# First expert layer: activations transposed in 64-row pieces, two row halves of the array at once, into one pair of banks

## Chip, cores and metric

One core of a Trainium2 chip runs the whole program. The metric is the device time of one execution in microseconds (us); lower is better. All data is float32 unless a row says otherwise.

## What is computed

A small network over 8 x 192 tokens of width 192: an embedding, a recurrent layer, a first mixture of experts, a linear attention and a second mixture of experts. The change lies in the first mixture of experts, whose reference, cut to what matters, is

```python
def _L0_ffn_ref(x, router_w, router_b, w1, b1, w2, b2):     # x: 1536 tokens x 192
    ...
    topk_probs, topk_idx = jax.lax.top_k(probs, 2)          # 2 of 8 experts for each token
    ...
    for e in range(NUM_EXPERTS):
        h = jax.nn.gelu(flat_x @ w1[e] + b1[e], approximate=False)   # 192 -> 288
        y = h @ w2[e] + b2[e]                                        # 288 -> 192
        out = out + y * gates[:, e:e + 1]
```

## The kernel before, in words

The kernel is written engine by engine; each engine's instructions run in the order of its code, and engines wait for each other through semaphores (`wait_ge`, `then_inc`). The first expert stage is `experts(0, ...)` on each engine. The routed rows (3072 of them, padded for each expert to whole groups of 64) are worked through in 28 tiles (`NT0`) of 128 rows. The lower 64 rows of a tile belong to one expert, the upper 64 rows to the same or another one.

For tile `i` the steps are:

- GpSimd gathers the tile's 128 rows of 192 numbers into one of four places of `xs` (line 747).
- `t_x(i)` on TensorE (lines 1982 to 2003) turns them over, in two transposes of 128 rows x 96 columns (line 1988); tiles alternate between bank 0 and bank 1. VectorE copies the result to `xTs` (`evac_x`, line 1608).
- `g1` (lines 2012 and 2015) multiplies by the first weights. The 64 rows of the one expert use the array's columns 0 to 63, those of the other columns 64 to 127; two such matmuls run as a pair. ScalarE applies gelu (line 1033).
- `t_h(i)` (line 2038) turns the 288 hidden numbers over, in three transposes of 128 x 96; tiles alternate between banks 4 and 5. VectorE copies to `hTs` (`evac_h`, line 1633).
- `g2` (lines 2058 and 2061) multiplies by the second weights, VectorE copies the 192 results out (`evac_y`, line 1642), and GpSimd scatters them to DRAM (line 755).

The order on TensorE is written out by hand (lines 2086 to 2096). An iteration `i` is `t_x(i + 3)`, `t_h(i)`, `g1(i + 2)`, `g2(i - 1)`; the last iterations lack `t_x`, and the last two `g1`. On VectorE an iteration is `evac_x(i + 3)`, `evac_h(i)`, `evac_y(i - 1)` (lines 1659 to 1665). On ScalarE it is a copy of the upper half's first weights (line 1064), gelu, and a copy of the upper half's second weights (line 1073). On GpSimd it is the gather of tile `i + 7`, then the scatter of tile `i` (lines 781 to 784). TensorE's sequencer also loads each tile's expert number (line 1980).

The second expert stage, `experts(1, ...)`, already turns its rows over in 64-row pieces, in `t_x`'s other branch (line 1999): piece `a` lies in array rows 64a to 64a + 63 and writes bank `a` of a pair of neighbouring banks, `two_banks[...]`. A tile name such as 64\*96 in the profile says how many array rows and columns an instruction uses: 128\*96 uses all rows, 96\*64 half the columns, 64\*96 and 64\*128 half the rows.

After the stage everything waits for its last scatter: the rows are read back (`load_acc`, line 552), and normalization, attention and the second expert stage follow.

Of the kernel before, what the change touches and what calls it, by code (L numbers as in the profile page):

```python
# [33 lines left out]
P = 128  # L34
# [5 lines left out]
KC = 96  # L40
NK = D // KC
# [8 lines left out]
GR = 64  # L50
NT0 = -(-(NTOK * TOPK // GR + NE - 1) * GR // P)
# [26 lines left out]
C_ID, C_IOTA, C_MASK = 0, P, 2 * P  # L78
# [23 lines left out]
def build(nc, x, out):  # L102
    ctx = ExitStack()
    with ctx:
# [29 lines left out]
        con = sb("con", [P, NCONST])  # L134
        ident = con[:, C_ID:C_ID + P]
# [68 lines left out]
        xTs = sb("xTs", [P, 2, NK, P])  # L204
# [138 lines left out]
        hact2 = carve(reg3, HID1).rearrange("p (b f) -> p b f", b=2)  # L343
        hTs = carve(reg3, HID1).rearrange("p (b f) -> p b f", b=2)

        hT2 = reg3[:, 0:2 * HID1].rearrange("p (b f) -> p b f", b=2)
        xs = carve(reg3, RING * D2).rearrange("p (s n) -> p s n", s=RING)
# [3 lines left out]
        bank = [psum[:, 512 * i:512 * (i + 1)] for i in range(8)]  # L351
        two_banks = [psum[:, 1024 * i:1024 * (i + 1)].rearrange("p (s c) -> p s c", s=2) for i in range(4)]
# [66 lines left out]


        X_BANKS = (0, 2)

        Y_BANKS = ((6, 7), (0, 1))

# [769 lines left out]
        def _(dve):  # L1194
            link = Chain(dve, dve_self)
            V = nc.vector
# [130 lines left out]
            for r, (minus, plus) in enumerate(((1, 4), (6, 9), (8, 2))):  # L1327
                s = (r + 2) % 3
                V.tensor_tensor(entries(0, minus), S.vv[:, r], S.qk[:, s], ALU.subtract)
                ins = V.tensor_tensor(entries(0, plus), S.vv[:, r], S.qk[:, s], ALU.add)  # L1330
# [269 lines left out]
            def experts(l, hid, hc):  # L1600
                nhc = hid // hc

                def evac_x(i, p):

                    dve.wait_ge(tx_mm, l * NT0 + i + 1)
                    if l == 0:
                        src = bank[p][:, 0:2 * P].rearrange("p (k t) -> p k t", k=NK)
                        V.tensor_copy(xTs[0:KC, p, :, :], src[0:KC]).then_inc(tx_ev, 1)  # L1608
                    else:
                        dst = xT64[:, p, :, :].rearrange("p k (s t) -> p k s t", s=2)  # L1610
                        src = two_banks[X_BANKS[i == 1]]

                        row = xs[:, i % RING, DX:D2]
                        link(V.tensor_tensor(gs[:, i:i + 1], row[:, 0:1], sel[:, 0, i:i + 1], ALU.mult))
                        V.scalar_tensor_tensor(out=gs[:, i:i + 1], in0=row[:, 1:2], scalar=sel[:, 1, i:i + 1],
                                               in1=gs[:, i:i + 1], op0=ALU.mult, op1=ALU.add)
                        for k in range(NK3):
                            ins = V.tensor_scalar(dst[:, k], src[:, :, 64 * k:64 * k + 64], gb2[:, 0, k:k + 1],  # L1618
                                                  gb2[:, 1, k:k + 1], ALU.mult, ALU.add)
                        ins.then_inc(tx_ev, 1)  # L1620

                def copy_w(i, p):


                    e = dve.value_load(et[0:1, i:i + 1], min_val=0, max_val=NE - 1)
                    V.tensor_copy(w1r[:, p, 0:W1R // 2],
                                  w1b.rearrange("p e f -> p (e f)")[:, bass.ds(e * W1R, W1R // 2)]
                                  ).then_inc(w1r_dve, 1)

                def evac_h(i, p):  # L1630

                    dve.wait_ge(th_mm, l * NT0 + i + 1)
                    V.tensor_copy(hTs[0:hc, p, 0:nhc * P], bank[4 + p][0:hc, 0:nhc * P]).then_inc(th_ev, 1)

                def evac_y(i):
                    s = i % YRING
                    dve.wait_ge(g2_mm, l * NT0 + i + 1)
                    if i >= YRING:

                        dve.wait_ge(scat[s], 16 * turns(l, i, YRING))  # L1640
                    if l == 0:
                        V.tensor_copy(ys[:, s, :], bank[6 + i % 2][:, 0:D]).then_inc(y_ev, 1)  # L1642
                    else:
                        y0, y1 = (bank[b][:, 0:D] for b in Y_BANKS[i == NT - 1])
                        link(V.tensor_scalar(ys[:, s, :], y0, gs[:, i:i + 1], None, ALU.mult))  # L1645
                        V.scalar_tensor_tensor(out=ys[:, s, :], in0=y1, scalar=gs[:, i:i + 1],
                                               in1=ys[:, s, :], op0=ALU.mult, op1=ALU.add).then_inc(y_ev, 1)

                if l:
                    dve.wait_ge(ld_ffn1, 16 * 4 * NE)  # L1650
                for p in range(2):
                    if l:
                        copy_w(p, p)
                    evac_x(p, p)

                if l == 0:

                    evac_x(2, 0)
                    for i in range(NT0):
                        if i + 3 < NT0:  # L1660
                            evac_x(i + 3, (i + 1) % 2)
                        evac_h(i, i % 2)
                        if i >= 1:
                            evac_y(i - 1)
                    evac_y(NT0 - 1)
                    return

                for i in range(NT):
                    if i + 2 < NT:
                        evac_x(i + 2, i % 2)  # L1670
                        copy_w(i + 2, i % 2)
                    evac_y(i)
# [194 lines left out]
        def _(pe):  # L1867
# [105 lines left out]
            def experts(l, hid, hc, w1, w2, biased):  # L1973
                nhc = hid // hc
# [7 lines left out]
                def t_x(i):  # L1982

                    s = i % RING
                    pe.wait_ge(xs_ready[s], 16 * (turns(l, i, RING) + 1))
                    if l == 0:
                        for k in range(NK):
                            ins = nc.tensor.transpose(bank[s % 2][0:KC, k * P:(k + 1) * P],
                                                      xs[:, s, k * KC:(k + 1) * KC], ident)
                    else:  # L1990


                        if i >= 2:
                            pe.wait_ge(tx_ev, NT0 + (i if i > 2 else 1))
                        dst = two_banks[X_BANKS[i == 1]]
                        for k in range(NK3):
                            for a in range(2):
                                rs = slice(64 * a, 64 * a + 64)
                                ins = nc.tensor.transpose(
                                    dst[:, a, 64 * k:64 * k + 64],  # L2000
                                    xs[rs, s, 64 * k:64 * k + P],
                                    con[rs, C_ID + 64 * a:C_ID + 64 * a + 64])
                    ins.then_inc(tx_mm, 1)
# [29 lines left out]

                def t_h(i, p):

                    pe.wait_ge(act_done, l * NT0 + i + 1)
                    for c in range(nhc):
                        ins = nc.tensor.transpose(bank[4 + p][0:hc, c * P:(c + 1) * P], hact2[:, p, c * hc:(c + 1) * hc], ident)
                    ins.then_inc(th_mm, 1)

                def g2(i, p, e):
# [515 lines left out]
```

## Time and profile before

| | |
|---|---|
| runs | 447.07, 447.06, 449.86 us; median 447.07 |
| the profiled execution, its own time | 444.51 us |
| its span, first to last instruction | 442.7 us |
| granted TensorE clock, mean | 0.97 of full speed |
| busy share of the span | TensorE 93%, weight loads 68%, VectorE 65%, ScalarE 52%, GpSimd 50% |
| the first expert stage in the span | about 135.5 us (first transpose) to 218 us (last scatter landed) |

A row of the timeline gives the start in the span, the duration, engine, line, operation, output and inputs, and a count; rows of one line that follow each other are merged, and then the duration goes from the first start to the last end. Brackets give idle time before the instruction and what ended it. PE is TensorE, PEld its weight loads, DVE VectorE, ACT ScalarE, POOL GpSimd. Matmul durations overlap, since the next matmul starts while the one before drains; what a matmul costs is read from the distance between starts. A float32 matmul appears as two matmuls in the trace, a transpose as one.

### The profile page before, as it was taken

The page shows a single profiled execution, that of the slowest core. Times are in us where ns is not written, and L with a number is a line of the kernel's source. Part 1 is how long each engine was busy: PE and PEld are TensorE (multiplying, and loading weights), DVE is VectorE, ACT ScalarE, POOL GpSimd, SP SyncE. Part 2 cuts the span into 40 slices and gives each one's busy share as a digit, 9 for nine tenths or more (in the row PEclk, how much of TensorE's full clock was granted, in tenths as well). Part 3 has the DMA queues.
Part 4 walks back from the last instruction along what each step waited for, and adds up shares of the span by engine and source line. Part 5 has one row for each costly group of instructions (what it writes and reads, how often), then busy time and mean ns, then how long its engine had stood idle before and what let it go on. Part 6 is the DMA issues. An engine that isn't in the chain of part 4 may idle for free.

```text
span 442.7 us, 10871 instructions
## 1 busy us (share of the span) xinstructions
PE 411.5 (93%) x3803; PEld 302.7 (68%) x3803; DVE 288.7 (65%) x1345; ACT 230.6 (52%) x427; POOL 219.5 (50%) x260
## 2 busy tenths in 40 slices
PE   9999998989879999999889889968999999999993
PEld 6653755637535666666534469635999999999993
DVE  6789999999883444444496248995465565565651
ACT  1487845441764555555235203754666666665650
POOL 5303797798045677774400001425556657566534
PEclk9999699999989999999889999988999999999998
DMA  8709300010132222221299993093233333333313
GB/s 234 107 17 250 69 1 2 1 36 1 64 112 62 64 72 73 72 72 44 87 293 230 225 224 117 18 191 108 52 53 54 58 62 52 60 59 52 51 21 36
DMA packets 38584, 38.27 MB, mean 86 GB/s; under 512 B 7331, under 2 KB 35793, under 8 KB 38517
## 3 DMA queue, kind: packets, MB, share of 16 engines
q1 hardware_dynamic: 27601, 22.84, 22.5%
q0 software_dynamic: 9024, 13.44, 16.0%
q10 hardware_dynamic: 1906, 1.30, 1.0%
q8 instruction: 31, 0.51, 0.5%
q14 instruction: 22, 0.18, 0.1%
HBM read 27.72 MB, written 10.53 MB: 86 GB/s over the span
## 4 chain that ended last, share of the span: by engine, by line
DMA 23%; PE 12%; DVE 8%; issue 5%; ACT 2%; POOLq 1%; POOL 1%; DVEq 0%; ACTq 0%
DMA out<-a,idx 21%; PE bank L2029 2%; DVE h L1701 2%; PE bank L2308 1%; PE bank L1874 1%; PE bank L2068 1%; DVE st L1218 1%; PE bank L2417 1%; PE bank L2340 1%; DMA a<-expert_rows 1%; PE bank L2314 1%; PE bank L2389 1%; ACT reg L1022 1%; PE bank L2362 1%; POOL out L767 1%
## 5 line engine op out<-in xcount | busy, mean ns | idle before, releaser
L767 POOL DMA_INDIRECT out<-a,idx x31 | 50.7, 1634 | 46.3 <-DMA out<-a,idx 32.7
L747 POOL DMA_INDIRECT reg<-xn_rows,idxs x59 | 57.7, 978 | 29.4 <-issue 16.2
L2029 PE MATMUL bank<-reg,xT 64*128 64x128 f32 x1116 | 69.0, 275 | 1.3 <-DVE reg L1618 1.3
L2029 PEld LDWEIGHTS bank<-reg,xT 64*128 64x128 f32 x1116 | 65.0, 188 | 1.4 <-DVE reg L1618 1.4
L2068 PE MATMUL bank<-reg 64*128 64x192 f32 x744 | 65.4, 323 | 0.0
L2068 PEld LDWEIGHTS bank<-reg 64*128 64x128 f32 x744 | 59.8, 187 | 0.0
L1874 PE MATMUL bank<-con 128*128 128x512 bf16 x201 | 54.1, 428 | 0.0
L1054 ACT ACTIVATE reg<-reg 128x1152 f32 x31 | 36.1, 1163 | 33.8 <-PE bank L2068 33.8
L1645 DVE TENSOR_SCALAR a<-bank,gs 128x192 f32<-128x192 f32 x31 | 12.9, 417 | 53.3 <-PE bank L2068 53.3
L1874 PEld LDWEIGHTS bank<-con 128*128 128x128 bf16 x201 | 21.4, 110 | 27.3 <-issue 11.5
L755 POOL DMA_INDIRECT expert_rows<-a,idx x28 | 27.6, 987 | 22.0 <-DVE a L1642 21.7
L1642 DVE COPY a<-bank 128x192 f32<-128x192 f32 x28 | 10.0, 357 | 40.7 <-PE bank L2061 40.7
L1073 ACT ACTIVATE xT<-reg 97x576 f32 x28 | 19.1, 682 | 31.1 <-PE bank L2061 31.1
L2012 PE MATMUL bank<-reg,xTs 96*64 (+1 forms) x112 | 33.2, 419 | 0.4 <-DVE xTs L1608 0.4
L2015 PE MATMUL bank<-xT,xTs 96*64 96x288 f32 (+1 forms) x112 | 33.2, 419 | 0.0
L1618 DVE TENSOR_SCALAR reg<-bank,gb 128x128 f32<-128x128 f32 x93 | 32.3, 403 | 0.0
L2058 PE MATMUL bank<-reg 96*64 x168 | 31.9, 326 | 0.0
L2061 PE MATMUL bank<-xT,reg 96*64 96x192 f32 x168 | 31.9, 326 | 0.0
L716 POOL TENSOR_TENSOR reg<-reg 128x128 f32<-128x128 f32 x63 | 26.1, 454 | 5.2 <-PE bank L2189 4.9
L796 POOL TENSOR_SCALAR onep<-rs 128x3 f32<-128x3 f32 x4 | 0.9, 230 | 56.0 <-DVE nm L1230 56.0
L2058 PEld LDWEIGHTS bank<-reg 96*64 96x64 f32 x168 | 22.7, 136 | 7.7 <-issue 0.4
L1037 ACT ACTIVATE reg<-bank 128x384 f32<-128x384 f32 x31 | 15.2, 491 | 18.9 <-PE bank L2029 18.9
(370 smaller groups left out, 880.1 us busy)
## 6 DMA issues: line engine op xcount, KB each, us to landing
reg<-in_w2b SPq DMA_DIRECT2D x8, 576.0 KB, 10.6
reg<-in_w1b SPq DMA_DIRECT2D x8, 288.0 KB, 10.7
reg<-in_w1a SPq DMA_DIRECT2D x8, 216.0 KB
reg<-in_w2a SPq DMA_DIRECT2D x8, 216.0 KB
xn_rows<-xn SPq DMA_DIRECT2D x4, 384.0 KB, 2.8
reg<-in_w1b SPq DMA_DIRECT2D x8, 192.0 KB, 8.2
xn_rows<-xn SPq DMA_DIRECT2D x1, 1152.0 KB, 7.2
out<-h SPq DMA_DIRECT2D x1, 1152.0 KB
```

The lines of the kernel that those rows point to most:

```text
L747: pool.indirect_dma_start(xs[:, i % RING, 0:(D, D2)[l]], None, xd[l], bass.IndirectOffsetOnAxis(ap=idxs[:, i:i + 1], axis=0)).then_inc(xs_ ...
L755: pool.indirect_dma_start(ybuf, bass.IndirectOffsetOnAxis(ap=idx2[:, i:i + 1], axis=0), ys[:, i % YRING, :], None).then_inc(scat[i % YRING ...
L767: pool.indirect_dma_start(out, bass.IndirectOffsetOnAxis(ap=idx2[:, i:i + 1], axis=0), ys[:, i % YRING, :], None, compute_op=ALU.add).then ...
L1054: nc.scalar.activation(w2r[:, p, :], w2b.rearrange("p e c n -> p (e c n)")[:, bass.ds(e * W2R, W2R)], ACT.Copy).then_inc(w2r_act, 1)
L1618: ins = V.tensor_scalar(dst[:, k], src[:, :, 64 * k:64 * k + 64], gb2[:, 0, k:k + 1], gb2[:, 1, k:k + 1], ALU.mult, ALU.add)
L1874: MM(bank[bk][:, :], con[:, 0:P // 2].bitcast(BF16), con[:, 0:2 * P].bitcast(BF16), start=True, stop=True)
L2012: MM(bank[2 + p][0:GR, 0:hid], xTs[0:r, p, k, 0:GR], w1v[0:r, bass.ds(e * (NK * hid) + k * hid, hid)], start=(k == 0), stop=(k == NK - 1))
L2015: ins = MM(bank[2 + p][GR:P, 0:hid], xTs[0:r, p, k, GR:P], w1u[0:r, i % 3, k * hid:(k + 1) * hid], start=(k == 0), stop=(k == NK - 1))
L2029: ins = MM(bank[2 + 2 * p + a][:, c * P:(c + 1) * P], w1r[rs, p, col:col + hc], xT64[rs, p, k, :], start=(c == 0 and k == 0), stop=(c == n ...
L2058: MM(bank[6 + p][0:GR, 0:D], hTs[0:r, p, c * P:c * P + GR], w2v[0:r, bass.ds(e * (nhc * D) + c * D, D)], start=(c == 0), stop=(c == nhc - 1))
L2061: ins = MM(bank[6 + p][GR:P, 0:D], hTs[0:r, p, c * P + GR:(c + 1) * P], w2u[0:r, i % 2, c * D:(c + 1) * D], start=(c == 0), stop=(c == nhc ...
L2068: ins = MM(bank[Y_BANKS[i == NT - 1][a]][:, 0:D], hT2[rs, p, c * P:(c + 1) * P], w2r[rs, p, c * D:(c + 1) * D], start=(c == 0), stop=(c == ...
```

## The change

Each transpose of the first stage becomes two: the lower 64 rows in array rows 0 to 63, the upper 64 rows in array rows 64 to 127, each against its own 64 x 64 part of the identity, with 64 moving columns instead of 128. The lower halves write the first bank of a pair, the upper halves the second. The rows use banks 0 and 1 for every tile but tile 1, which uses banks 4 and 5; the hidden values use banks 4 and 5 for every tile. Where tiles took turns at two places, there is now one place, so `t_x(i)` waits for the copy of the tile before, and so does `t_h(i)`. VectorE's two copies keep their sizes, and read both banks in pieces of 64.

```diff
         X_BANKS = (0, 2)
+        XF_BANKS = (0, 2)
+        H_BANKS = 2
...
                     if l == 0:
-                        src = bank[p][:, 0:2 * P].rearrange("p (k t) -> p k t", k=NK)
-                        V.tensor_copy(xTs[0:KC, p, :, :], src[0:KC]).then_inc(tx_ev, 1)
+                        src = two_banks[XF_BANKS[i == 1]][0:KC, :, 0:NK * GR].rearrange("p s (k t) -> p k s t", k=NK)
+                        V.tensor_copy(xTs[0:KC, p, :, :].rearrange("p k (s t) -> p k s t", s=2), src).then_inc(tx_ev, 1)
...
-                    V.tensor_copy(hTs[0:hc, p, 0:nhc * P], bank[4 + p][0:hc, 0:nhc * P]).then_inc(th_ev, 1)
+                    V.tensor_copy(hTs[0:hc, p, 0:nhc * P].rearrange("p (c s t) -> p c s t", c=nhc, s=2),
+                                  two_banks[H_BANKS][0:hc, :, 0:nhc * GR].rearrange("p s (c t) -> p c s t", c=nhc)
+                                  ).then_inc(th_ev, 1)
...
                     if l == 0:
+                        if i >= 2:
+                            pe.wait_ge(tx_ev, i if i > 2 else 1)
+                        dst = two_banks[XF_BANKS[i == 1]]
                         for k in range(NK):
-                            ins = nc.tensor.transpose(bank[s % 2][0:KC, k * P:(k + 1) * P],
-                                                      xs[:, s, k * KC:(k + 1) * KC], ident)
+                            for a in range(2):
+                                rs = slice(GR * a, GR * a + GR)
+                                ins = nc.tensor.transpose(dst[0:KC, a, GR * k:GR * k + GR],
+                                                          xs[rs, s, k * KC:(k + 1) * KC],
+                                                          con[rs, C_ID + GR * a:C_ID + GR * a + GR])
...
                 def t_h(i, p):
 
-                    pe.wait_ge(act_done, l * NT0 + i + 1)
+                    pe.wait_ge(act_done, i + 1)
+                    if i >= 1:
+                        pe.wait_ge(th_ev, i)
                     for c in range(nhc):
-                        ins = nc.tensor.transpose(bank[4 + p][0:hc, c * P:(c + 1) * P], hact2[:, p, c * hc:(c + 1) * hc], ident)
+                        for a in range(2):
+                            rs = slice(GR * a, GR * a + GR)
+                            ins = nc.tensor.transpose(two_banks[H_BANKS][0:hc, a, GR * c:GR * c + GR],
+                                                      hact2[rs, p, c * hc:(c + 1) * hc],
+                                                      con[rs, C_ID + GR * a:C_ID + GR * a + GR])
                     ins.then_inc(th_mm, 1)
```

On TensorE, one iteration in the steady part of the stage, before (line 1980 loads the expert number, 1988 is `t_x`, 2038 is `t_h`, 2012 and 2015 are `g1`):

```order
L1980 TENSOR_LOAD et
L1980 ISA x2
L1988 MATMUL bank<-con,reg 96x128 [waits xs_ready1]
L1988 MATMUL bank<-con,reg 96x128
L2038 MATMUL bank<-con,reg 96x128 [waits act_done]
L2038 MATMUL bank<-con,reg 96x128 x2
L2012 ISA [waits w1r_act,tx_ev]
```

The same place in the changed kernel (1997 is `t_x`, 2052 is `t_h`, 2022 begins `g1`):

```order
L1984 TENSOR_LOAD et
L1984 ISA x2
L1997 MATMUL bank<-con,reg 96x64 [waits tx_ev,xs_ready1]
L1997 MATMUL bank<-con,reg 96x64 x3
L2052 MATMUL bank<-con,reg 96x64 [waits th_ev,act_done]
L2052 MATMUL bank<-con,reg 96x64 x5
L2022 ISA [waits w1r_act,tx_ev]
```

Five transposes of 128 columns have become ten of 64, the first of each group has one more wait, and nothing else on the engine has another place.

Near the start of the stage on TensorE, the third tile's transposes and the products of the second tile behind them, before:

```order
L1988 MATMUL bank<-con,reg 96x128 [waits xs_ready2]
L1988 MATMUL bank<-con,reg 96x128
L2012 ISA [waits w1r_act,tx_ev]
L2012 MATMUL bank<-reg,xTs 64x288
L2015 MATMUL bank<-xT,xTs 64x288
```

And in the changed kernel:

```order
L1997 MATMUL bank<-con,reg 96x64 [waits tx_ev,xs_ready2]
L1997 MATMUL bank<-con,reg 96x64 x3
L2022 ISA [waits w1r_act,tx_ev]
L2022 MATMUL bank<-reg,xTs 64x288
L2025 MATMUL bank<-xT,xTs 64x288
```

This is the first place with the new wait (here for the first tile's copy); the first two tiles have two different pairs of banks and wait for their rows alone, as before.

## Rows read from the trace of the kernel before

**Rows 1.** Spans and granted clock of the core

```profile
core 0: 442.7 us, clock 0.970
```

**Rows 2.** Busy time by stretch: us, each engine busy (instructions), granted clock, DMA share, GB/s

```profile
140.00:150.00 10.00, 10.00 (x89) 6.51 (x88) 4.42 (x12) 5.00 (x10) 4.91 (x5) 1.00 0.17 52
...
190.00:200.00 10.00, 10.00 (x95) 6.72 (x92) 3.99 (x10) 5.67 (x12) 7.04 (x8) 1.00 0.25 70
```

**Rows 3.** Timeline of TensorE, one iteration of the stage's steady part

```profile
168.53 0.33 PE L2058 MATMUL bank<-reg 97*64 x1
...
168.70 0.32 PE L2058 MATMUL bank<-reg 97*64 x1
...
168.96 0.42 PE L1988 MATMUL bank<-con,reg 128*96 128x128 f32 x2
169.22 0.49 PE L2038 MATMUL bank<-con,reg 128*96 128x128 f32 x3
169.64 0.46 PE L2012 MATMUL bank<-reg,xTs 96*64 x1
...
170.67 0.33 PE L2058 MATMUL bank<-reg 96*64 x1
...
171.75 0.42 PE L1988 MATMUL bank<-con,reg 128*96 128x128 f32 x2
```

**Rows 4.** The stage's transposes by line: duration in ns min/median/max, first and last start

```profile
L1988 PE MATMUL bank<-con,reg x56: 272/273/316, 135.7 to 205.3; 128*96 128x128 f32 x56
...
L2038 PE MATMUL bank<-con,reg x84: 272/273/317, 139.6 to 212.3; 128*96 128x128 f32 x84
```

**Rows 5.** Timeline of the other engines in the same iteration

```profile
169.08 0.36 DVE L1642 COPY a<-bank 128x192 f32<-128x192 f32 x1 [1.55 <-PE bank L2061]
169.42 0.42 DVE L1608 COPY xTs<-bank 96x256 f32<-96x256 f32 x1
169.72 0.99 POOL L755 DMA_INDIRECT expert_rows<-a,idx  x1 [0.52 <-DVE a L1642]
169.76 0.54 DVE L1633 COPY reg<-bank 96x384 f32<-96x384 f32 x1
170.41 0.39 ACT L1033 ACTIVATE reg<-bank 128x288 f32<-128x288 f32 x1
171.01 0.97 POOL L747 DMA_INDIRECT reg<-xn_rows,idxs  x1 [0.30 <-issue]
```

**Rows 6.** Timeline at the stage's two ends, and the chain that ended last behind it

```profile
136.72 0.45 PE L2012 MATMUL bank<-reg,xTs 96*64 x1 [0.39 <-DVE xTs L1608]
212.08 0.54 PE L2038 MATMUL bank<-con,reg 128*96 128x128 f32 x3
...
212.55 0.38 PE L2058 MATMUL bank<-reg 96*64 x1
...
215.70 2.34 DMA expert_rows<-a,idx
```

**Rows 7.** Second expert stage: its 64-row transposes, timeline and durations in ns

```profile
312.25 0.35 PE L1999 MATMUL bank<-con,reg 64*128 64x64 f32 x6
312.44 2.23 PE L2029 MATMUL bank<-reg,xT 64*128 64x128 f32 x36
...
L1999 PE MATMUL bank<-con,reg x186: 216/222/274, 304.1 to 425.7; 64*128 64x64 f32 x186
```

**Rows 8.** Attention: matmuls of 64 rows by 96 columns, timeline and durations in ns

```profile
256.35 0.59 PE L2368 MATMUL bank<-reg 64*96 64x102 f32 x8
256.87 1.32 PE L2340 MATMUL bank<-reg 128*96 128x256 f32 x5
...
L2368 PE MATMUL bank<-reg x32: 245/248/325, 247.4 to 270.4; 64*96 64x102 f32 x32
```

**Rows 9.** DMA issues: queue, operation, count, median us from issue to landing

```profile
reg<-xn_rows,idxs POOLq DMA_INDIRECT x59, 2.8
```

## The prediction

> **What bounds the kernel now.** First the granted clock of the whole span: 0.970, so the TensorE clock is rarely held back [rows 1]. Then the stretches of the first expert stage: TensorE is busy in all of 10 us out of 10, at clock 1.00 (the 2.4 GHz level), while VectorE has 4.0 to 4.4, ScalarE 5.0 to 5.7 and GpSimd 4.9 to 7.0; the stretches between these two read alike [rows 2]. So TensorE ends last in this stage, and what counts is the distance between the starts of its instructions. One iteration, from `t_x` to the next `t_x`, goes from 168.96 to 171.75, 2.78 us [rows 3]. The other engines' rows of the same iteration show that each waits for TensorE: VectorE sits idle 1.55 us for `g2`, GpSimd 0.52 us for the copied results [rows 5]. Behind the stage the chain that ended last goes through its last scatter [rows 6], and all that follows hangs on that; so a microsecond saved on TensorE here should come out at the end of the program.
>
> **What an iteration's transposes cost.** From the first start of `t_x` to the first start of `g1` it is 169.64 - 168.96 = 0.68 us [rows 3]. Inside, from merged rows: the two of `t_x` last 0.42 from the first start to the second's end, and one lasts 0.272 [rows 4], so the second starts at 169.11, 0.15 behind the first; `t_h` starts 0.11 later; its three last 0.49, so its two inner distances are (0.49 - 0.273)/2 = 0.109 each. `g1` starts 0.20 behind the last. So the pace is 0.109 per transpose, five make 0.545, and 0.135 is paid for entering (0.04) and leaving (0.09). Before them it is 0.26 from the last pair of `g2`, against 0.17 within `g2` [rows 3], again 0.09 more.
>
> **What they will cost.** Five transposes become five pairs of half the rows and half the moving columns. The trace has such pairs: in the second expert stage six pieces (three pairs) take from 312.25 to 312.44 up to the next line's start, 0.19, or 0.063 a pair; their own starts, (0.35 - 0.222)/2 = 0.064 a pair, agree [rows 7]. That is the dear end for a pair; the cheap end is half of 0.109, 0.054, if only the moving columns count. The pieces here hold 96 columns and not 128, so I go between: 0.060. The cost of entering and leaving I leave as it is: the attention's matmuls on 64 rows by 96 columns sit between other shapes, and leave for the next with (0.59 - 0.248)/3 = 0.114 a pair at most inside, the last starting at 256.69, and 256.87 - 256.69 = 0.18 behind it, 0.09 above the 0.087 that 102 columns need by 0.109 x 102/128 [rows 8]. It is the same 0.09 as here. So each transpose saves 0.109 - 0.060 = 0.049 us, and an iteration five of these, 0.245: 2.78 becomes 2.54.
>
> **The sum.** There are 56 transposes in `t_x` and 84 in `t_h` [rows 4], 140. The two of tile 1 lie in the shadow of VectorE's first copy, for which `g1` of tile 0 waits 0.39 us [rows 6]. In the last iterations `t_h` stands alone, 0.47 from its start to `g2`, and TensorE goes on without a gap there too [rows 6]. So 138 x 0.049 = 6.8 us; with 0.063 it is 138 x 0.046 = 6.3, with 0.054 it is 7.6.
>
> **The added waits cost nothing.** `t_x(i + 3)` now waits for `evac_x(i + 2)`, queued behind it `t_h`, `g1` and `g2` of the iteration. That copy begins at 169.42 and ends at 169.84, the next `t_x` is at 171.75: 1.9 us to spare, about 1.7 when the iteration is 0.24 shorter. `t_h(i)` waits for `evac_h(i - 1)`, done at 169.76 + 0.54 = 170.30 [rows 5], and the next `t_h` is at about 172.00, 1.7 to spare, about 1.4 after the change. VectorE's two copies keep their elements but read two banks in pieces of 64; no row shows that for a plain copy. Whatever they gain is hidden behind TensorE; were they twice as long, 0.42 + 0.54 = 0.96 more, both waits would still be met. At the start, `t_x(2)` waits for a copy that `g1(0)` waited for already. At nothing I also put gelu: it ends at 170.80 for a `t_h` at 172.00 [rows 5].
>
> **GpSimd comes close.** A gather and a scatter, with the 0.30 us that stands before a gather counted for both, take 0.97 + 0.30 + 0.99 + 0.30 = 2.56 [rows 5], against the new 2.54. It would fall back 0.02 an iteration, under half a microsecond over the 20 or so tiles that are still gathered. The scatter at 169.72 is of the tile `i` whose `g2` ended the iteration before 168.96, which `t_x(i + 4)` began at 166.18; the gather behind it at 171.01 is of tile `i + 8`, turned over four iterations later, at 177.31. 6.3 us less the 2.8 to landing [rows 9] leaves 3.5; three shorter iterations take 0.7 of it. If TensorE got down to the cheap end, 2.51, GpSimd would lose 0.05 an iteration, 1 us in all, still covered. Behind the last gather it has only scatters, and catches up.
>
> **One rule that speaks against it.** In the second stage's rows three pairs, each with two loads of 128 columns, pass in 0.19 us [rows 7]. The Trainium skill's "TensorE: Matmul & The Clock Gate", in its section on LDWEIGHTS, says that loading the stationary operand takes its columns divided by 1.2, in ns, whatever the rows. By it a pair of 96-column pieces would not go under 80 ns, even with both loads side by side: 138 x (0.109 - 0.080) = 4.0 us saved and 443.1 in place of 440.3. For the second stage's 128 columns it would give 107 ns a pair, where 63 was measured; so the trace disagrees for transposes, as far as three pairs tell.
>
> **Rivals.**
> Weight loads set the pace. Halved rows and columns leave ten loads for five, and only the moving columns got shorter, so loads may no longer hide. For it: the 64 x 96 matmuls of the attention take 0.52 from first start to the next line, for four pairs, and 0.114 a pair inside [rows 8]; five pairs would be 0.52 + 0.11 = 0.63 against 0.68, three pairs 0.41 against 0.47. That saves 25 x 0.05 + 3 x 0.06 = 1.4 us: 445.7. Against it: those stream 102 columns a pair, which alone needs 0.087, and the pieces of rows 7 are faster than that.
>
> The gain is larger: entering and leaving get cheaper too, and the whole 0.68 shrinks to five pairs at 0.063, 0.32. That is 0.36 an iteration, 2.42; 25 x 0.36 + 3 x 0.28 = 9.8 us: 437.3, less about 0.5 if GpSimd, at 2.56, then holds back the last gathers. Against it: the 0.09 on leaving stands in rows 3 and 8 alike.
>
> Slower: the two halves don't run side by side. Place: the ten pieces of an iteration. One after the other, each would pay its 0.060 and the 0.04 of a load that the piece before doesn't hide: 0.100, two of them 0.200 against 0.109, 138 x 0.091 = 12.6 us: 459.7. It decides from a pace of 0.054 per single piece on. Against it: rows 7 have 0.032 per piece.
>
> No gain at the end: TensorE saves its 6.8 us, but the stage's end or what follows gives back 5 or more, by the last scatters or by a later stretch that falls differently against the clock: about 445.5. Nothing in the chain behind the stage speaks for it; it starts from the last scatter [rows 6].
>
> **How the numbers follow.** The profiled execution took 444.51 us, 1.8 more than its span; the median of the runs shown is 447.07. The saving lies inside the span and is carried over as it is: 447.07 - 6.8 = 440.3. Chances: forecast 0.70, larger gain 0.07, weight loads 0.12, no gain at the end 0.06, slower 0.05. The forecast's own range is 439.0 to 441.5 by the pair's bounds and half a microsecond of scatter between runs. The range for 8 in 10 reaches 437.5 (the larger gain) to 443.6 (past the skill's rule), leaving out most of the loads' case, the lost gain and the slower one. About 1%, 4.5 us, is what a measurement of this kernel can tell from no change. Faster by more: 0.70 + 0.07, less 0.02 for a forecast that comes out short: 0.75. Within 1%: the loads, the lost gain and that 0.02: 0.20. Slower: 0.05.
>
> **What would show it.** After the change, an iteration of 2.54 us between starts of `t_x`; ten pieces in five pairs with 0.06 between pairs; 0.43 to 0.45 from the first piece to `g1`; no idle time of TensorE put down to VectorE's two copies in the steady part; GpSimd's wait of 0.52 before a scatter shrunk to about 0.30; the last scatter some 6.8 us earlier, and the second expert stage shifted by the same. Pairs 0.085 or more apart would say that loads set the pace; pieces 0.05 or more apart singly, that halves don't overlap; waits before `t_x` or `t_h` on VectorE, that one place is too few. A last scatter 6.8 us earlier with an unchanged time would say that the gain was lost later.

## The result, and the profile after

The changed kernel takes 440.75 us at the median of 4 runs (437.76 to 443.02), the one before 447.06 beside it (445.98 to 449.86): a ratio of 0.986, with a 95% interval of 0.982 to 0.990. The forecast was 440.3. A second comparison with more rounds, told below, gives 439.58 against 446.67, 7.1 us less. The ratios, here and below, leave out runs that took over 1.5% more than the fastest run of the same kernel (three of the ten of hidden_only, one of the six of two_tiles_start).

In the changed kernel 1997 is the line of `t_x`, 2052 of `t_h`, 2022 and 2025 are `g1`, 2074 and 2077 `g2`; 1610, 1635 and 1646 are VectorE's copies of rows, hidden values and results; 749 and 757 are GpSimd's gather and scatter. The timeline of TensorE from one group of transposes to the next:

```profile
161.56 0.32 PE L2074 MATMUL bank<-reg 97*64 x1
...
161.82 0.32 PE L1997 MATMUL bank<-con,reg 64*96 64x64 f32 x4
161.97 0.33 PE L2052 MATMUL bank<-con,reg 64*96 64x64 f32 x6
162.24 0.46 PE L2022 MATMUL bank<-reg,xTs 96*64 x1
```

The next `t_x` is at 164.34, so the iteration is 2.52 us where it was 2.78 [rows 3], and from the first piece to `g1` it is 162.24 - 161.82 = 0.42 where it was 0.68. The start lies 0.26 behind the last pair of `g2`, as before. The other engines in the same iteration:

```profile
161.66 0.97 POOL L749 DMA_INDIRECT reg<-xn_rows,idxs  x1 [0.30 <-issue]
161.94 0.36 DVE L1646 COPY a<-bank 128x192 f32<-128x192 f32 x1 [1.37 <-PE bank L2077]
162.21 0.41 DVE L1610 COPY xTs<-bank 96x256 f32<-96x256 f32 x1
162.54 0.54 DVE L1635 COPY reg<-bank 96x384 f32<-96x384 f32 x1
162.94 0.99 POOL L757 DMA_INDIRECT expert_rows<-a,idx  x1 [0.30 <-issue]
```

GpSimd no longer waits for VectorE's copied results (0.52 in [rows 5]): only its 0.30 of "issue" is left between a gather and a scatter. VectorE still sits idle 1.37 us for `g2` (1.55 before), and its two copies, now in pieces of 64, last as long as before.

All waits of TensorE for other engines in the whole stage (engine and line, what for; sum in us, times, longest) are one row, the start of the first tile, which was there before [rows 6]:

```profile
PE bank L2022 <- DVE xTs L1610: 0.5, 1, 0.5
```

The chain that ended last still goes through the last scatter:

```profile
211.93 2.33 DMA expert_rows<-a,idx
```

It starts at 211.93 instead of 215.70 [rows 6]. That is 3.8 us earlier and not 7, because in this one execution the stage began later: its first transpose is at 139.23, 3.5 us behind the 135.7 of [rows 4]. Nothing before the stage was changed. Two stretches ahead of it, of the changed kernel (columns as in [rows 2]):

```profile
45.00:60.00 15.00, 15.00 (x64) 9.85 (x65) 14.93 (x105) 10.42 (x23) 11.53 (x15) 0.66 0.16 36
105.00:130.00 25.00, 21.96 (x109) 13.88 (x107) 20.69 (x128) 11.28 (x23) 8.80 (x12) 0.86 0.25 74
```

and the same stretches of the kernel before:

```profile
45.00:60.00 15.00, 15.00 (x69) 10.03 (x70) 14.93 (x104) 10.25 (x22) 11.73 (x15) 0.77 0.17 39
105.00:130.00 25.00, 19.32 (x127) 11.59 (x126) 21.10 (x121) 14.68 (x30) 7.66 (x9) 0.98 0.24 74
```

The granted clock was a mixture of its two levels (1.2 GHz would read 0.50), lower in this execution than in that: 0.66 against 0.77 and 0.86 against 0.98, and the same work got less far (64 and 109 matmuls where there were 69 and 127). The control experiment below, the same changed kernel once more, has 0.77 and 0.99 there and begins the stage at 136.04. So the profiled execution (441.41 us, span 439.6) shows 3.1 us of the gain, and the stage itself shows all of it.

For that reason the experiments are read by one measure besides the time: the length of the stage, from the first start of `t_x` to the landing of the last scatter, in the one profiled execution of each kernel. Every row is read from its timeline:

| kernel | stage begins | stage | one iteration | stage's end to the second stage's first transpose | profiled execution |
|---|---|---|---|---|---|
| before | 135.7 | 82.3 | 2.78 | 86.0 | 444.51 |
| after | 139.2 | 75.0 | 2.52 | 86.7 | 441.41 |
| rows_only | 136.1 | 82.9 | 2.81 | 85.8 | 445.10 |
| hidden_only | 136.2 | 81.2 | 2.76 | 85.1 | 442.84 |
| one_place | 135.9 | 82.3 | 2.78 | 89.6 | 448.05 |
| half_by_half | 136.4 | 75.1 | 2.52 | 87.1 | 439.05 |
| one_half | 134.7 | 82.6 | 2.79 | 86.8 | 444.33 |
| pieces_twice | 137.4 | 82.7 | 2.80 | 86.6 | 446.92 |
| copies_twice | 136.3 | 76.8 | 2.52 | 85.4 | 438.83 |
| as_changed | 136.0 | 75.0 | 2.52 | 87.0 | 438.60 |
| two_tiles | 137.4 | 73.5 | 4.75 for two tiles | 88.4 | 439.60 |
| two_tiles_start | 136.3 | 73.4 | 4.75 for two tiles | 85.8 | 435.81 |

The two stretches outside the stage scatter by 4 to 5 us between executions of the same code, in no order that goes with the kernels; the stage repeats (75.0 in both executions of the changed kernel).

### The profile page after: what moved, and what is told of

Read it like the earlier page. It is cut to its first block, busy times and chain, and to the rows that moved or that the text cites. A ratio compares the mean times of both kernels' runs of the same rounds, so it can differ in the third digit from the quotient of the medians.

```text
span 439.6 us, 11204 instructions
## 1 busy us (share of the span) xinstructions
PE 410.0 (93%) x3943; PEld 302.2 (69%) x3943; DVE 286.7 (65%) x1345; ACT 230.9 (53%) x427; POOL 219.3 (50%) x260
## 4 chain that ended last, share of the span: by engine, by line
DMA 23%; PE 12%; DVE 8%; issue 5%; ACT 2%; POOLq 1%; POOL 1%; DVEq 0%; ACTq 0%
DMA out<-a,idx 21%; PE bank L2039 2%; DVE h L1705 2%; PE bank L2324 1%; PE bank L2084 1%; DVE st L1220 1%; PE bank L1878 1%; PE bank L2433 1%; PE bank L2356 1%; PE bank L2378 1%; DMA a<-expert_rows 1%; PE bank L2330 1%; PE bank L2405 1%; ACT reg L1024 1%; PE bank L2384 1%
## 5 line engine op out<-in xcount | busy, mean ns | idle before, releaser
L1878 PE MATMUL bank<-con 128*128 128x512 bf16 x201 | 56.2, 441 | 0.0
```

The costliest lines, as they stand in the source:

```text
L1878: MM(bank[bk][:, :], con[:, 0:P // 2].bitcast(BF16), con[:, 0:2 * P].bitcast(BF16), start=True, stop=True)
```

## The experiments

The theory: pairs of halves run side by side, each transpose saves about 0.05 us, and the entering and leaving of a block of transposes stay as they were. It was tested part by part.

**Do the parts add up?** rows_only cuts only `t_x` and its copy (with its wait and banks) as the change does; `t_h` stays whole with its two places. hidden_only does the other half. Against the kernel before, rows_only is

```diff
+                        if i >= 2:
+                            pe.wait_ge(tx_ev, i if i > 2 else 1)
+                        dst = two_banks[XF_BANKS[i == 1]]
                         for k in range(NK):
+                            for a in range(2):
+                                rs = slice(GR * a, GR * a + GR)
+                                ins = nc.tensor.transpose(dst[0:KC, a, GR * k:GR * k + GR],
...
```

and hidden_only

```diff
+                    if i >= 1:
+                        pe.wait_ge(th_ev, i)
                     for c in range(nhc):
+                        for a in range(2):
+                            rs = slice(GR * a, GR * a + GR)
+                            ins = nc.tensor.transpose(two_banks[H_BANKS][0:hc, a, GR * c:GR * c + GR],
...
```

each with the matching copy of the change's diff.

> The stage is measured from its first transpose's start to the landing of its last scatter: 82.30 us before (135.74 to 218.04), 75.02 in the changed kernel (139.23 to 214.25); an iteration between starts of t_x is 2.78 and 2.52. Here only t_x is in halves. Theory (halves side by side, each transpose on the path saves the same 0.053): 54 x 0.053 = 2.8 saved, stage 79.5, iteration 2.67. Rival (the gain lies in entering and leaving the block, since its first or last member is now a short piece): entering by t_x's piece and leaving by t_h's whole transpose, so about half of it or nothing, by which end it is, and not two fifths; iteration 2.65 or 2.78.

> Only t_h in halves. Theory: 84 x 0.053 = 4.4 saved, stage 77.9, iteration 2.62, and the two parts alone sum to the whole 7.3. Rival (gain at the ends of the block): iteration 2.65 or 2.52, and the parts don't sum by the counts 54 and 84. Whole transposes before the pieces add one change of shape inside the block: if that costs the 0.09 to 0.13 of the other changes, iteration 2.72.

Measured: rows_only 446.90 us against 446.93, ratio 1.002 (0.999 to 1.005), so nothing; hidden_only 444.39, ratio 0.993 (0.989 to 0.996). The theory's iteration of 2.67 for rows_only was missed by far: 2.81, longer than before. Its 2.62 for hidden_only was missed too: 2.76, close to the 2.72 that the expectation gave to one more change of shape inside the block. The parts do not add up: one stage is 0.6 us longer and the other 1.1 shorter, where the whole change makes it 7.3 shorter. (The medians of hidden_only differ by 2.5 us; what goes beyond the stage's 1.1 lies outside the stage and is not explained.) The timeline of TensorE says where it went. rows_only, where line 1995 is `t_x`, 2046 `t_h` and 2020 `g1`:

```profile
166.70 0.32 PE L1995 MATMUL bank<-con,reg 64*96 64x64 f32 x4
166.95 0.53 PE L2046 MATMUL bank<-con,reg 128*96 128x128 f32 x3
167.41 0.46 PE L2020 MATMUL bank<-reg,xTs 96*64 x1
```

and hidden_only, with 1992, 2046 and 2016:

```profile
166.44 0.42 PE L1992 MATMUL bank<-con,reg 128*96 128x128 f32 x2
166.80 0.37 PE L2046 MATMUL bank<-con,reg 64*96 64x64 f32 x6
167.10 0.46 PE L2016 MATMUL bank<-reg,xTs 96*64 x1
```

The whole block is 0.71 and 0.66. Five halved transposes made 0.68 into 0.42, 0.053 each. Two of them should give 0.68 - 0.105 = 0.575, three 0.68 - 0.158 = 0.52; both blocks are 0.135 longer than that. It lies at the border inside the block: `t_h` begins 0.36 behind `t_x` in hidden_only and 0.26 in the kernel before, with the same two whole transposes between. This 0.135 is just the 0.09 for leaving plus the 0.04 for entering that the prediction read at the ends of the block. Between a whole transpose and a halved one they are paid once more. So it is the change of shape that costs, not the beginning of transposes. The Trainium skill's "TensorEngine Tiling (Array Packing)", section Tiling Modes, says that switching the tiling mode drains the engine, without a price; the trace agrees in that a switch costs time, and 0.135 is the price here.

**Does one place cost anything?** one_place keeps whole transposes and takes only the shared bank with its waits.

```diff
-                        src = bank[p][:, 0:2 * P].rearrange("p (k t) -> p k t", k=NK)
+                        src = bank[int(i == 1)][:, 0:2 * P].rearrange("p (k t) -> p k t", k=NK)
...
+                        if i >= 2:
+                            pe.wait_ge(tx_ev, i if i > 2 else 1)
...
+                    if i >= 1:
+                        pe.wait_ge(th_ev, i)
                     for c in range(nhc):
-                        ins = nc.tensor.transpose(bank[4 + p][0:hc, c * P:(c + 1) * P], hact2[:, p, c * hc:(c + 1) * hc], ident)
+                        ins = nc.tensor.transpose(bank[4][0:hc, c * P:(c + 1) * P], hact2[:, p, c * hc:(c + 1) * hc], ident)
```

> Transposes of 128 rows as before, but one bank for the rows (another for tile 1) and one for the hidden values, with the changed kernel's waits. Theory (the waits are met long before): stage 82.3, iteration 2.78, no idle time of TensorE put down to VectorE's copies, time as before within 1%. Rival (one place costs, and ate a part of the gain): iteration over 2.80, stage over 83.

Measured: 446.58 us, ratio 1.000 (0.997 to 1.003), stage 82.3 as before. Neither new wait is ever late while VectorE's copies have their usual length.

**Does the order of issue matter?** half_by_half issues all lower pieces of a tile and then all upper ones.

```diff
-                        for k in range(NK):
-                            for a in range(2):
+                        for a in range(2):
+                            for k in range(NK):
...
-                    for c in range(nhc):
-                        for a in range(2):
+                    for a in range(2):
+                        for c in range(nhc):
```

> The changed kernel with the pieces in another order: in t_x and in t_h first all lower halves, then all upper ones. Theory (two pieces overlap only if neighbours lie in different halves): t_x's four pieces are 2 + 2 and t_h's six 3 + 3 with one overlap at each change of half; of ten pieces six or seven have a distance of 0.054 or more in place of five, so 0.05 to 0.15 more an iteration, 2.57 to 2.67, stage 76.5 to 79. If nothing overlaps: ten distances of 0.054, iteration 2.78, stage 82.3. Rival (the gain comes from shorter pieces, whatever their order): iteration 2.52, stage 75.0.

Measured: 439.51 us, ratio 0.986 (0.981 to 0.991), iteration 2.52. The 2.57 to 2.67 expected of an issue in strict order was missed; the block is the same:

```profile
164.05 0.32 PE L1997 MATMUL bank<-con,reg 64*96 64x64 f32 x4
164.21 0.34 PE L2052 MATMUL bank<-con,reg 64*96 64x64 f32 x6
164.47 0.46 PE L2022 MATMUL bank<-reg,xTs 96*64 x1
```

**Do the halves run side by side at all?** one_half takes all ten pieces from the lower half of the array; the upper 64 rows of each tile are not transposed, their places get the lower ones' values.

```diff
-                                rs = slice(GR * a, GR * a + GR)
+                                rs = slice(0, GR)
...
-                                                          con[rs, C_ID + GR * a:C_ID + GR * a + GR])
+                                                          con[rs, C_ID:C_ID + GR])
```

> The changed kernel with every piece read from the lower 64 rows, through the lower half of the array; the upper 64 rows of each tile aren't transposed (the lower ones stand in for them). The run with the halves one after the other took 2.52 us an iteration like the changed kernel, which leaves two readings. Theory (a half takes its pieces in order, but doesn't wait for pieces that were issued earlier to the other half, so both halves are at work whatever the order): here ten distances of 0.051, 0.26 more, iteration 2.77, stage 82. Rival (nothing overlaps, a piece of 64 rows simply costs 0.026 wherever it lies): iteration 2.52, stage 75.0.

Measured: 444.33 us in one run (before: 446.53), iteration 2.79, stage 82.6, against 75.0 with both halves.

```profile
165.26 0.43 PE L1997 MATMUL bank<-con,reg 64*96 64x64 f32 x4
165.53 0.49 PE L2052 MATMUL bank<-con,reg 64*96 64x64 f32 x6
165.95 0.46 PE L2022 MATMUL bank<-reg,xTs 96*64 x1
```

The six pieces of `t_h`, 0.216 each, last 0.49 from the first start to the last end, so single pieces of one half come every (0.49 - 0.216)/5 = 0.055. With two halves a whole pair comes in that time. Together with half_by_half this also says that a piece of the upper half does not wait for lower pieces issued before it: in half_by_half the lower pieces alone need 0.055 each, and the upper ones added nothing.

The first starts show it directly. These are the pieces that began within 0.03 us of a `t_x`'s first start, in half_by_half:

```profile
164.05 0.27 PE L1997 MATMUL bank<-con,reg 64*96 64x64 f32 x2
```

and in one_half:

```profile
165.26 0.26 PE L1997 MATMUL bank<-con,reg 64*96 64x64 f32 x1
```

In half_by_half the first two pieces issued are both lower ones, and one_half shows that a half alone begins only one in that time. So one of the two that began is an upper piece, and it started ahead of the second lower piece, which was issued before it.

**Do the weight loads set the pace?** pieces_twice issues every piece twice, so that a block is ten pairs and not five.

```diff
-                        for k in range(NK):
+                        for k in (0, 1, 0, 1):
...
-                    for c in range(nhc):
+                    for c in (*range(nhc), *range(nhc)):
```

> The changed kernel with each block of pieces issued twice (same values written again): five more pairs an iteration at an unchanged cost of entering and leaving. Theory (a pair costs 0.051): iteration 2.52 + 0.26 = 2.78, stage 82. Rival (weight loads set the pace in a longer run of pieces, 0.087 a pair as in the attention's matmuls): 2.52 + 0.43 = 2.95, stage 87.

Measured: 446.92 us in one run, iteration 2.80, 0.28 more for five more pairs, 0.056 a pair. The rival's 2.95 was missed.

```profile
168.00 0.43 PE L1997 MATMUL bank<-con,reg 64*96 64x64 f32 x8
168.27 0.50 PE L2052 MATMUL bank<-con,reg 64*96 64x64 f32 x12
168.70 0.46 PE L2022 MATMUL bank<-reg,xTs 96*64 x1
```

Six pairs last 0.50 here, as long as six single pieces in one_half (0.49).

**How much may the copies grow?** copies_twice lets VectorE do both copies twice, the second alone releasing TensorE.

```diff
+                        link(V.tensor_copy(xTs[0:KC, p, :, :].rearrange("p k (s t) -> p k s t", s=2), src))
                         V.tensor_copy(xTs[0:KC, p, :, :].rearrange("p k (s t) -> p k s t", s=2), src).then_inc(tx_ev, 1)
...
+                    link(V.tensor_copy(dst, src))
+                    V.tensor_copy(dst, src).then_inc(th_ev, 1)
```

> The changed kernel with both of VectorE's copies run twice in a row, the second after the first has ended. Theory (one place is enough, some 1.4 us to spare for t_h): the copies end some 2.4 us behind the start of t_x, the next t_h comes at 2.69; iteration 2.52 to 2.56, stage 75 to 76. Rival (one place is near its limit): VectorE's 0.36 + 0.82 + 1.08 and the gaps between them reach over the iteration, 2.65 or more, with idle time of TensorE put down to VectorE.

Measured: 438.83 us in one run, and 2.52 per iteration in the steady part. VectorE's timeline there, with each copy in two rows and 0.33 us of slack before the next results:

```profile
170.54 0.41 DVE L1610 COPY xTs<-bank 96x256 f32<-96x256 f32 x1
170.99 0.42 DVE L1611 COPY xTs<-bank 96x256 f32<-96x256 f32 x1
171.33 0.54 DVE L1638 COPY reg<-bank 96x384 f32<-96x384 f32 x1
171.91 0.55 DVE L1639 COPY reg<-bank 96x384 f32<-96x384 f32 x1
172.79 0.36 DVE L1648 COPY a<-bank 128x192 f32<-128x192 f32 x1 [0.33 <-PE bank L2079]
```

The stage still grew by 1.8 us, at its two ends, where TensorE waited for the second copies (2024 is `g1`, 2054 `t_h`, 2076 `g2`; of these only `t_h`'s wait is new with the change):

```profile
PE bank L2024 <- DVE xTs L1611: 1.0, 1, 1.0
PE bank L2054 <- DVE reg L1639: 0.8, 2, 0.6
PE bank L2076 <- DVE reg L1639: 0.2, 1, 0.2
```

**The change once more.** as_changed is the changed kernel itself, in five rounds beside the version that follows.

> The changed kernel once more, unaltered. In its first profile the stage was 7.3 us shorter, but the whole execution only 3.1 us (444.51 to 441.41). Theory (the missing 4 us lie in stretches with the same instructions, where the granted clock fell otherwise in that execution): stage 75.0 again, iteration 2.52, and over many runs 7.3 off the time, a ratio of 0.984. Rival (the stretches behind the stage give some of it back each time): ratio 0.988 to 0.993.

Measured: 439.58 us against 446.67, ratio 0.985 (0.981 to 0.988); stage 75.0 again. The saving of 7.1 us and the stage's 7.3 agree.

**Fewer changes of shape.** If a change costs 0.135 and more, two tiles' transposes should stand in one block. two_tiles does this: `t_x` of two tiles, `t_h` of two, then `g1` of two and `g2` of two; the two tiles' pieces lie side by side in the same banks, the copies and ScalarE's work follow the order, and the gathers are issued two tiles earlier. The core of it:

```diff
-                    for i in range(NT0):
...
+                    for i in range(0, NT0, 2):
                         if i + 2 < NT0:
-                            e.append(expert_of(i + 2))
-                        if i + 3 < NT0:
-                            t_x(i + 3)
-                        t_h(i, i % 2)
+                            e += [expert_of(i + 2), expert_of(i + 3)]
+                        if i + 4 < NT0:
+                            t_x(i + 4)
+                            t_x(i + 5)
+                        t_h(i, 0)
+                        t_h(i + 1, 1)
                         if i + 2 < NT0:
-                            g1(i + 2, i % 2, e[i + 2])
...
+                            g1(i + 2, 0, e[i + 2])
+                            g1(i + 3, 1, e[i + 3])
+                        g2(i, 0, e[i])
+                        g2(i + 1, 1, e[i + 1])
```

> The changed kernel with the blocks of two tiles put together: eight pieces of t_x and twelve of t_h in a row, then two g1, then two g2, and gathers issued two tiles earlier. The array changes its shape half as often. Theory (entering and leaving a block costs about 0.27 us, once for two tiles now): 14 x 0.27 = 3.8 off the stage, 71 to 72, as long as GpSimd keeps up. Rival (GpSimd's 2.57 for a gather and a scatter, against 2.38 for TensorE, bounds the stage): 2.57 a tile in the second half, stage 73 to 74, with idle time of TensorE on gathered rows. If a change of shape costs nothing: 75.

Measured: 437.56 us against 446.53, ratio 0.978 (0.973 to 0.983). Two tiles take 4.75 us where two iterations took 5.04, 0.29 less. From the ends of one block, 0.09 before it, 0.04 entering and 0.09 leaving, 0.22 was to be had. Another 0.05 lies in `g1` (2036): behind a block the second pair starts 0.29 after the first, and the third 0.25 after the second; in the second tile's `g1`, which follows another `g1`, the second pair starts 0.24 after the first. That makes 0.27 of the 0.29, the price that the expectation gave to a block.

```profile
146.47 0.43 PE L2011 MATMUL bank<-con,reg 64*96 64x64 f32 x8
146.73 0.50 PE L2067 MATMUL bank<-con,reg 64*96 64x64 f32 x12
147.16 0.46 PE L2036 MATMUL bank<-reg,xTs 96*64 x1
...
147.45 0.41 PE L2036 MATMUL bank<-reg,xTs 96*64 x1
...
147.70 0.41 PE L2036 MATMUL bank<-reg,xTs 97*64 x1
...
148.19 0.41 PE L2036 MATMUL bank<-reg,xTs 96*64 x1
...
148.43 0.40 PE L2036 MATMUL bank<-reg,xTs 96*64 x1
```

14 blocks at 0.29 would be 4.1 us; the stage gave 75.0 - 73.5 = 1.5, so the 71 to 72 expected was missed. The rest went into waits, 2.6 us in all (2011 is `t_x`, 2089 `g2`):

```profile
PE bank L2011 <- DMA reg<-xn_rows,idxs: 1.9, 3, 0.9
PE bank L2089 <- DVE reg L1644: 0.7, 1, 0.7
```

Two of the three waits for gathered rows, 1.3 us, are those of the first tiles, which are now wanted earlier than their rows arrive. `g2` waits at the last tiles. The third wait for rows comes late in the stage, before the last tile's `t_x`:

```profile
194.90 0.32 PE L2011 MATMUL bank<-con,reg 64*96 64x64 f32 x4 [0.63 <-DMA reg<-xn_rows,idxs]
```

There GpSimd, at 2.57 us a tile against TensorE's 2.38, has used up its lead. This is the sign that the expectation named for its rival, and 73.5 lies in the rival's range; but up to that tile the distance stayed at 4.75 for two tiles, and the late rows cost 0.6 of the 2.6.

two_tiles_start puts `g1` of the first tiles between the first transposes, to give those rows time.

```diff
-                    for i in range(4):
-                        t_x(i)
+                    t_x(0)
+                    t_x(1)
                     g1(0, 0, e[0])
+                    t_x(2)
+                    t_x(3)
...
+                            if i == 0:
+                                t_x(4)
+                                t_x(5)
```

> The kernel with the blocks of two tiles, and the start of the stage put in another order: the first tile's g1 stands before the transposes of tiles 2 and 3, and those of tiles 4 and 5 behind g1 of tile 2, so that TensorE works while their rows are on the way. Theory (the stage lost 1.9 us at its start to three waits for gathered rows, less one more change of shape): stage 72.0 to 72.8 in place of 73.5, time 1 us under the other. Rival (GpSimd's 2.57 per tile bounds the stage in its second half, so that a faster start only moves the wait): stage 73.5 again, with idle time of TensorE on gathered rows late in the stage.

Measured: 438.63 us against 446.67, ratio 0.982 (0.977 to 0.986), stage 73.4: not better than two_tiles, and short of the 72.0 to 72.8 expected. The waits changed their names (2036 is `g1`, 2067 `t_h`):

```profile
PE bank L2089 <- DVE reg L1644: 0.7, 1, 0.7
PE bank L2036 <- DVE xTs L1618: 0.6, 1, 0.6
PE bank L2011 <- DMA reg<-xn_rows,idxs: 0.6, 1, 0.6
PE bank L2067 <- ACT reg L1035: 0.2, 1, 0.2
```

and nothing was won by it. In the first tiles the waits are 0.8 us instead of 1.3, but this order has two more blocks there than two_tiles, about 0.5 us by 0.27 each. The row of 2011 is again the last tile's, late in the stage, as the rival said; that a faster start would only lengthen this wait was not shown, since the start did not get faster. The two versions are not told apart by their intervals; two_tiles and the change itself differ by less than 1% too (ratios 0.978 and 0.985 against the same kernel), with a stage that is 1.5 us shorter behind it.

## Why the prediction was right

**A pair at 0.060.** Measured 0.056: 0.28 for five pairs in pieces_twice. It lies between the two ends given, 0.054 and 0.063, nearer the cheap one: half the rows and half the moving columns take half the time of a whole transpose, and the other half of the array works in the same time. That it is the columns that count was not tried by itself; the 0.114 at most for 64 rows with 102 columns [rows 8] suggests it. So a transpose saves 0.109 - 0.056 = 0.053, and 138 of them 7.3 us where 6.8 were forecast; the stage shrank by 82.3 - 75.0 = 7.3. This is the one term that was mis-sized, by 0.5 us.

**Entering and leaving unchanged.** Right in sum: with 0.04 and 0.09, and five pairs at 0.056, the block is 0.41, and 0.42 was measured. What the prediction did not see is that these two are the price of a change of shape, and so fall due inside the block as well when only one part is changed. [rows 7] had a sign of it: there the pieces stand before matmuls of the same shape 64\*128, and the next line starts 0.19 behind the first of three pairs, with nothing added for leaving. The forecast for the whole change didn't hang on it, but a forecast by parts (2 of 5 of the gain for the rows) would have been wrong, as the expectation of rows_only was.

**The waits at nothing.** Right for the steady part, and with a margin as stated: one_place 1.000, and copies twice as long left the iteration at 2.52. At the stage's ends the statement that, with copies twice as long, "both waits would still be met" was too wide: there `t_h` waited twice in copies_twice, 0.8 us in all. The copies themselves are not longer for reading two banks, as these rows of the changed kernel show (durations in ns, 28 each) beside the 0.42 and 0.54 of [rows 5], so the case did not arise:

```profile
L1610 DVE COPY xTs<-bank x28: 408/410/421, 139.6 to 202.5; 96x256 f32<-96x256 f32 x28
...
L1635 DVE COPY reg<-bank x28: 542/544/555, 143.3 to 208.9; 96x384 f32<-96x384 f32 x28
```

**GpSimd close, and covered.** Right. Gather and scatter follow each other at 2.57 us a tile against TensorE's 2.52, so GpSimd falls back 0.05 an iteration, as said for the cheap end. TensorE waited for no gathered row, and behind the last gather GpSimd waits for results again:

```profile
198.90 0.99 POOL L757 DMA_INDIRECT expert_rows<-a,idx  x1 [0.30 <-issue]
200.35 0.99 POOL L757 DMA_INDIRECT expert_rows<-a,idx  x1 [0.46 <-DVE a L1646]
202.87 0.97 POOL L757 DMA_INDIRECT expert_rows<-a,idx  x1 [1.53 <-DVE a L1646]
```

**The loads' rule.** The Trainium skill's "TensorE: Matmul & The Clock Gate", section LDWEIGHTS, gave an estimate of 80 ns a pair and 443.1 us. pieces_twice has 56 ns a pair over ten pairs on end, so the trace disagrees with it for these transposes, now with more than the three pairs of [rows 7]. With it falls the rival of the weight loads (0.114 a pair from the attention's rows), whose pairs would have stood at least 0.085 apart.

**Halves side by side.** The rival that forecast 459.7 named 0.054 per single piece as the point from which it decides, and single pieces of one half do cost 0.055 (one_half). But in the change the other half's piece comes in the same time, so its condition is not met.

**The gain at the end.** Right in the median (6.3 and 7.1 us in two comparisons). That the first median, 440.75, came within 0.5 us of the forecast is in part luck: its four runs lie between 437.76 and 443.02, and the 7.3 us of the stage would have made it 439.8. The prediction expected the second expert stage to be shifted by the same; in a single execution that can't be seen, as its distance from the first stage's end is anything from 85.1 to 89.6 us in the table. The granted clock before the stage differed between two executions of the changed kernel (rows above); that it explains the distance behind the stage as well was not tried.

## What to carry to other kernels

Count the changes of shape on the array as well as the instructions: halving some transposes among whole ones costs 0.135 us for one more change of shape inside a block here, and rows_only lost by that all it had saved. Convert neighbours together, or put those of one shape in one block, as two_tiles does. Where the stretches outside the changed stage scatter by more than half of the gain, as here, compare the length of the stage and the distance between repeats first, and the program's time by enough rounds.

## What had not been expected of the hardware

A piece on the upper half of the array starts beside pieces of the lower half that were issued before it: the order of issue made no difference (2.52 in both orders), while a half alone takes 0.055 per piece. The Trainium skill's "TensorE: Matmul & The Clock Gate", in the part on packing small matmuls, section The mechanism, says that matmuls start and end strictly in the order of the program. By that the lower pieces of half_by_half would have held back the upper ones and the iteration would be 2.57 to 2.67; with 2.52, and with two pieces begun within 0.03 us where a half alone begins one, the trace disagrees.

And a piece of half the rows and half the moving columns takes half the time of a whole transpose (0.055 of 0.109), not a quarter, so a single half gains nothing (one_half, 2.79): all the gain is the second half running in the same time.
